# Two-layer gated cross-attention with routed experts: the steps of layer 0's attention dealt anew over four units, the pick split in two

## The reference, cut to what matters

```python
def reference(x, ctx, g_xattn, g_ffn, ...):     # x 32 x 128 x 128, ctx 32 x 77 x 128, float32
    x = x + tanh(g_xattn[0]) * xattn0(layernorm(x), ctx)   # 8 heads of 64
    x = x + tanh(g_ffn[0])   * ffn0(layernorm(x))          # 8 experts, the best 2 of each token
    x = x + tanh(g_xattn[1]) * xattn1(layernorm(x), ctx)   # 16 heads of 8
    x = x + tanh(g_ffn[1])   * ffn1(layernorm(x))          # 8 experts, the best 2 of each token
    return x

def xattn0(x, c):
    q, k, v = x @ Wq, c @ Wk, c @ Wv
    return softmax(q k^T / 8) v @ Wo + bo                  # for each head

def ffn0(x):
    scores = x @ Wr.T + br
    w, (_, idx) = softmax(scores), top_k(scores + biases_N, 2)
    ...
```

## Time and profile before

| | |
|---|---|
| median of 3 runs | 753.79 us (753.32 to 755.35) |
| the profiled execution | 752.22 us, span 750.5 us |
| mean granted clock of PE | 0.934 of full speed |
| busy: PE, PEld | 629.7 (84%), 571.5 (76%) |
| busy: DVE, ACT, POOL | 557.5 (74%), 444.4 (59%), 448.3 (60%) |
| chain that ended last | PE 37%, DVE 27%, ACT 13%, issue 10%, POOL 6%, DMA 4%, SP's queue 3% |

### The profile page before, as it was taken

One profiled execution on the slowest core, in us unless ns is written; L12 is line 12 of the kernel. 1 busy time (PEld: TensorE's weight loads), 2 busy tenths in 40 slices (PEclk: granted clock), 3 DMA queues, 4 the chain that ended last, 5 costly groups with the idle time before them and its releaser, 6 DMA issues.

```text
span 750.5 us, 16523 instructions
## 1 busy us (share of the span) xinstructions
PE 629.7 (84%) x4501; PEld 571.5 (76%) x4501; DVE 557.5 (74%) x1971; ACT 444.4 (59%) x1275; POOL 448.3 (60%) x665
## 2 busy tenths in 40 slices
PE   6889787878776869998778998898879986799997
PEld 4668687868766869898767787787877876689885
DVE  3368688787876797997887888988868765455784
ACT  2477676766634546665657686677665742344462
POOL 4034347776766877886563435677656763766761
PEclk9599999999977899999989999999989995799999
DMA  9446667544523335335534533625414003333555
GB/s 258 132 116 163 179 169 201 140 115 129 146 76 93 93 102 154 104 101 156 146 100 102 126 96 70 137 78 103 120 34 117 25 28 87 101 93 100 148 167 162
DMA packets 127383, 89.48 MB, mean 119 GB/s; under 512 B 30996, under 2 KB 116276, under 8 KB 127260
## 3 DMA queue, kind: packets, MB, share of 16 engines
q1 hardware_dynamic: 110844, 64.93, 34.1%
q0 software_dynamic: 8128, 17.65, 7.2%
q10 hardware_dynamic: 8320, 5.85, 2.8%
HBM read 50.73 MB, written 39.85 MB: 121 GB/s over the span
## 4 chain that ended last, share of the span: by engine, by line
PE 37%; DVE 27%; ACT 13%; issue 10%; POOL 6%; DMA 4%; SPq 3%; DVEq 1%; ACTq 0%; POOLq 0%
PE banks L1162 8%; PE banks L1181 5%; PE banks L1025 4%; DVE row_max L1418 3%; POOL x_rows L1905 3%; PE banks L905 2%; SPq L815 2%; ACT prob L1294 2%; PE banks L968 2%; DVE prob L1421 2%; DVE x_res L1754 2%; PE banks L1010 2%; DMA v_rows<-vo 2%; ACT xm L1287 2%; POOL y_rows L1912 1%
## 5 line engine op out<-in xcount | busy, mean ns | idle before, releaser
L1912 POOL DMA_INDIRECT y_rows<-y_sb,result_at x134 | 131.0, 978 | 61.6 <-issue 24.6
L1162 PE MATMUL banks<-xb,up 128*128 128x128 f32 x820 | 123.4, 290 | 22.5 <-DVE hidden L1730 11.4
L1905 POOL DMA_INDIRECT x_rows<-xm,row x120 | 120.4, 1003 | 32.5 <-issue 27.5
L1162 PEld LDWEIGHTS banks<-xb,up 128*128 128x128 f32 x820 | 110.5, 203 | 32.7 <-issue 14.2
L1867 POOL TENSOR_TENSOR v_flat<-v_raw,row_head 104x64 f32<-104x64 f32 (+1 forms) x128 | 55.8, 464 | 73.1 <-ACT v_raw L1335 72.7
L1319 ACT ACTIVATE prob_t<-banks 128x512 f32<-128x512 f32 x192 | 73.3, 439 | 27.6 <-PE banks L992 27.6
L1025 PE MATMUL banks<-v_flat,prob_t 128*128 128x108 f32 (+2 forms) x640 | 86.9, 285 | 2.6 <-issue 1.7
L1025 PEld LDWEIGHTS banks<-v_flat,prob_t 128*128 128x128 f32 (+1 forms) x640 | 80.6, 199 | 9.6 <-ACT prob_t L1319 5.8
L1181 PE MATMUL banks<-down,hidden 128*128 x536 | 84.9, 283 | 0.1
L1833 POOL TENSOR_TENSOR prob<-prob,inv_sum 128x616 f32<-128x616 f32 x32 | 39.1, 1221 | 58.7 <-DVE inv_sum L1481 58.6
L1181 PEld LDWEIGHTS banks<-down,hidden 128*128 128x128 f32 x536 | 73.6, 199 | 0.5 <-issue 0.5
(11 more groups left out here) (238 smaller groups left out, 1630.4 us busy)
## 6 DMA issues: line engine op xcount, KB each, us to landing
vo_flat<-v_rows SPq DMA_DIRECT2D x32, 256.0 KB
x_norm<-x_rows SPq DMA_DIRECT2D x74, 72.0 KB
v_rows<-vo SPq DMA_DIRECT2D x38, 128.0 KB
x_far<-x_rows SPq DMA_DIRECT2D x60, 72.0 KB
gathered<-y_rows ACTq DMA_DIRECT2D x32, 128.0 KB
q_rows<-up_raw SPq DMA_DIRECT2D x8, 512.0 KB, 2.8
q_even<-q_rows SPq DMA_DIRECT2D x12, 256.0 KB
q_odd<-q_rows SPq DMA_DIRECT2D x12, 256.0 KB
```

Source lines behind the costliest of these rows:

```text
L1162: done = pe.matmul(banks[:, UP_BANK[i % 2], part * P:(part + 1) * P], block_w[:, i % WR, part // 2, part % 2 * P:(part % 2 + 1) * P], xb[: ...
L1905: pool.indirect_dma_start(out=x_rows[layer][:, :], out_offset=bass.IndirectOffsetOnAxis(ap=row[:, n, c:c + 1], axis=0), in_=xm[:, i % 2, j ...
L1912: pool.indirect_dma_start(out=y_rows[layer][:, :], out_offset=bass.IndirectOffsetOnAxis(ap=result_at[:, i % (2 * YR):i % (2 * YR) + 1], ax ...
```

## The change

It does three things, all in the plan; no instruction is added or taken away.

1. `prepare_attention0_at`: the key blocks of a group are dealt 3, 3, 2, 0 over turns 0 to 3 (they were 3, 2, 1 and, ahead of them, 2 in the turn 3 before). xt comes last in turn 2 instead of in its second place. The norm of a group goes from turn 0 to turn 2 of the group before, normalize from turn 1 to turn 3.
2. `value_halves`: the unit of each four that makes two half blocks of values is now turn 3 and no longer turn 2.
3. `route_tasks`: every group has steps of its own, and `pick` is cut in two. Its second half is `count`: DVE's hot vectors, their sum and the counts, and POOL's two products. In layer 0, mnorm, mnormalize, mturn, route and pick of groups 0 to 4 come one unit later, count one after pick, rank and the scatters two units later than before (the scatters of the groups 3 and 4 are then pressed into two units). Groups 5 to 7 and all of layer 1 keep their units, with count right behind pick.

So turn 0 then has three k0, mnormalize and count; turn 1 three k0, rank, mturn and a scatter; turn 2 two k0, xt, norm, route, lead and two scatters; turn 3 two value halves, normalize, pick, mnorm and a scatter. The tables of group 4 (totals, blocks, block_bias) go from units 27, 28 and 29 to 29, 30 and 31.

```diff
     at = {}
-    usual = steps[0]
     for g in range(NG):
         u = spacing * g + lag
-        steps_of = steps[g - NG + 4] if NG - 3 <= g < NG - 1 else usual
-        for kind, step in zip(("mnorm", "mnormalize", "mturn", "route", "pick", "rank", "lead"), steps_of[0]):
+        steps_of = steps[g]
+        for kind, step in zip(("mnorm", "mnormalize", "mturn", "route", "pick", "count", "rank", "lead"), steps_of[0]):
...
-        n = min(max(2 * (last + 1), (5 * (u + 1) + 13) // 4), 2 * CTX_BLOCKS)
+        n = min(max(2 * (last + 1), (5 * (u + 1) + 12) // 4), 2 * CTX_BLOCKS)
...
     g = (u + 1) // GS + 1 if u >= GS - 1 else 1
-    if g >= NG:
-        return [], [], [], []
-    keys = ((3, 2, 1, 2) if g > 1 else (3, 3, 2, 0))
     turn = u % GS
-    before = sum(keys[i] for i in ((3, 0, 1, 2) if g > 1 else (0, 1, 2))[:(turn + 1) % GS if g > 1 else turn])
-    places = [[("k0", g, before + n)] for n in range(keys[turn])]
-    if turn == 2:
+    keys = (3, 3, 2, 0)
+    places = [[("k0", g, sum(keys[:turn]) + n)] for n in range(keys[turn])] if g < NG else []
+    if turn == 2 and g < NG:
         places.append([("xt", g)])
     places += [[]] * (3 - len(places))
-    return places + [[("norm", g)] if turn == 0 else [("normalize", g)] if turn == 1 else []]
+    norms = [("norm", 1)] if u == 0 else [("normalize", 1)] if u == 1 else []
+    if turn == 2 and g + 1 < NG:
+        norms = [("norm", g + 1)]
+    if turn == 3 and g < NG:
+        norms = [("normalize", g)]
+    return places + [norms]
...
-            if late and late[0] == ("expert_w",):
+            if late and late[0][0] in ("count", "expert_w"):
...
-    tasks = [route_tasks(0, GS, 6, ((range(7), (5, 6, 7, 8)), (range(7), (5, 6, 7, 8)), ((0, 1, 2, 3, 3, 4, 5), (5, 5, 5, 5)))),
...
+    tight = ((0, 1, 2, 3, 4, 4, 5, 6), (5, 6, 7, 8))
+    spread0 = (1, 2, 3, 4, 5, 6, 7, 8)
+    steps0 = [(spread0, (7, 8, 8, 9))] * 3 + [(spread0, (7, 7, 8, 8))] * 2 + [tight, ((0, 1, 2, 3, 3, 3, 4, 5), (5, 5, 5, 5)), tight]
...
+    tasks = [route_tasks(0, GS, 6, steps0), route_tasks(1, 2 * GS, 13, steps1)]
...
+                elif kind == "count":
+                    layer, g = t[1:]
+                    i = layer * NG + g
+                    s = i % 2
+                    w.wait_ge("top_idx", (GS + 1) * (i + 1))
+                    w.wait_ge("constants", N_CONSTANTS)
                     iota3 = iota8[:, :].unsqueeze(1).to_broadcast([P, GS, NEXP])
                     for n in (0, 1):
                         dve.tensor_tensor(hot[:, s, n, :, :], iota3, top_idf[:, s, :, n:n + 1].to_broadcast([P, GS, NEXP]),
...
-                elif kind == "pick" and t[1] == 0:
+                elif kind == "count" and t[1] == 0:
```

More of the change, by code:

```diff
@@ L361, in order @@
     out += first[1:] + [("wvo", 0), ("wvo", 1), ("ctx", 1), ("v0", 0, 0), ("v0", 0, 1), ("gates",)]
-    tasks = [route_tasks(0, GS, 6, ((range(7), (5, 6, 7, 8)), (range(7), (5, 6, 7, 8)), ((0, 1, 2, 3, 3, 4, 5), (5, 5, 5, 5)))),
-             route_tasks(1, 2 * GS, 13, (((0, 1, 3, 5, 6, 7, 9), (9, 11, 13, 15)), ((0, 1, 3, 5, 6, 7, 9), (8, 9, 10, 11)),
-                                         ((0, 1, 2, 3, 4, 5, 6), (6, 6, 7, 7))))]
+    tight = ((0, 1, 2, 3, 4, 4, 5, 6), (5, 6, 7, 8))
+    spread0 = (1, 2, 3, 4, 5, 6, 7, 8)
+    steps0 = [(spread0, (7, 8, 8, 9))] * 3 + [(spread0, (7, 7, 8, 8))] * 2 + [tight, ((0, 1, 2, 3, 3, 3, 4, 5), (5, 5, 5, 5)), tight]
+    spread1 = (0, 1, 3, 5, 6, 6, 7, 9)
+    steps1 = [(spread1, (9, 11, 13, 15))] * 5 + [(spread1, (8, 9, 10, 11)), ((0, 1, 2, 3, 4, 4, 5, 6), (6, 6, 7, 7)), (spread1, (9, 11, 13, 15))]
+    tasks = [route_tasks(0, GS, 6, steps0), route_tasks(1, 2 * GS, 13, steps1)]
     after0 = [[("expert", 1, e)] for e in range(NEXP)] + first_keys_and_queries()
```

## The result

Slower, and by three times what was forecast: 778.08 us (median of 6 runs, 775.75 to 781.78) against 753.56 for the kernel before on the same chip, ratio 1.0327 [1.0287, 1.0367]. That is +24.5 us where +8.0 stood, outside the range (748 to 767). The profiled execution took 781.78 us with a span of 780.0; it is the slowest of its six, so differences of the traces run a little high (29.6 us against 24.5).

A forecast was written before the change was run, and what follows sets the result against it. Layer 0's attention was taken to run at VectorE's pace plus its waiting gaps. Terms +8.6 (units 12 to 26), 0, -1.4 and +0.8 made +8.0 us on 752.22: 760.2, stated as a 761.5 median, range 748 to 767.

The forecast's parts named there:

- The mechanism of turn 1: Layer 0 attention, turn 1: late exponentials, third key block, then rank and mturn in bank 7; 5.3 to 7.95 us, +2.7.
- its rows are read 0.73 later ... and row_max comes 1.51 later: Turn 1, units 17 and 25: rank from 5.9, read 0.73 later, mturn at 6.9, row_max 1.51 later, at 8.4 us.
- Turn 2: Layer 0 attention: two key blocks, xt's low half, norm, route and lead; 7.4 to 7.25 us, -0.15 a group.
- Turn 0: Layer 0 attention: no late start of ACT, count and shift added; -1.25 us a group, then +0.7 for POOL.
- The wait for POOL's power: Turn 0: normalize's shift waits for POOL's power until 6.35 us after row_max, where 5.65 was wanted; +0.7 a group.
- an exclusive lock: VectorE and GpSimd's shared ports: rank gains outside POOL's divide; 761.5 us by this rule, 765.5 without it.
- Turn 3: Layer 0 attention: loses key blocks, rank and mnormalize, gains pick and mnorm; 5.2 to 5.55 us, +0.3 a group.
- Units 2 to 11: Early units with little or no routing: gains and losses cancel, 0 us, between -3 and +2.
- Units 27 to 30: End of the stage: same work, lighter units 27 and 28 close a fifth of the idle time; -1.4 us.
- The term for block_bias in unit 31: Block_bias comes ahead of rank on PE and in bank 7; its read and one rank cost +0.8 us.
- Closing gaps: Rival: PE and ACT run ahead in lighter turns 3 and 0, turn 1 5.9 us; 746 to 751.5 us, chance 0.25.
- POOL falling behind: Rival: late divides hold PE's turning of the probabilities, 1.5 us more a group; 767 us, chance 0.1.

The follow-up runs named there:

- second trace of the changed kernel: The changed kernel run again unaltered, on the other kind of chip: 829.9 us against 803.3 for the kernel before, ratio 1.0323.
- the split kernel: Kernel before with only the count taken out of the pick, same steps, count right behind it: 801.4 us against 802.7, ratio 1.0008.
- norm late: Changed kernel with the shifting and scaling of xm moved behind the following unit's exponentials: 822.0 us, ratio 1.0241 to the kernel before.
- rank late: Changed kernel with rank, turning, totals and blocks moved behind the following unit's scores and exponentials: 820.3 us, ratio 1.0197 to the kernel before.
- filling the first stand: Changed kernel with the transposes of the probabilities made three times over in turn 1, nothing moved: 824.9 us, ratio 1.0249 to the kernel before.
- cutting the second: Changed kernel with layer 0's turning, route and rank in the bank the last split did not use: 825.3 us, ratio 1.0272 to the kernel before.

## Why the prediction was wrong

- *The mechanism of turn 1* was right to a few tenths: exponentials 2 us late, rank at 5.71 in the heavy unit (forecast 5.9), the chain rank, turning, scores, and 17 and 25 longer than 13 and 21. **The step that failed is "its rows are read 0.73 later ... and row_max comes 1.51 later".** These prices were taken from rows at full clock. In the place where I put them they measured 1.23 and 2.66 at half clock, so 1.65 more a unit, 6.6 in four units; turn 1 came out 6.1 above the forecast (38.0 for units 13, 17, 21 and 25, forecast 31.9). The rows on record did not say that the clock would fall: 0.73 was measured behind a stand of 2.92 us and 1.51 behind one of 1.26, both at full clock, and the 0.84 of unit 12 comes from its first 2 us. But the same trace has unit 23, where PE stands 2.88 us ahead of the rank, and the scores behind it run at half clock. Windows of before, in units 12, 15 and 23:

```profile
107.92:109.92 2.00, 2.00 (x11) 2.00 (x11) 1.27 (x4) 1.88 (x6) 1.38 (x2) 0.50 0.67 202
131.90:133.67 1.77, 1.77 (x14) 1.77 (x15) 0.94 (x6) 0.00 (x0) 1.23 (x2) 1.00 0.04 8
182.00:184.06 2.06, 2.06 (x9) 2.06 (x9) 0.92 (x5) 0.69 (x2) 1.23 (x3) 0.50 0.70 188
```

  So a second sum at half clock was called for, and was not made.
- *Turn 2*: 8.0 us in the mean instead of 7.25, 3.0 in four units. It begins at half clock (unit 18: 0.51 from 161.98 to 163.60, 1.00 behind it): x_res waits for the weighted sum four times, 3.3 us in all.
- *Turn 0*: 7.34, 7.81 and 7.34 instead of 6.45, 3.1 us. The wait for POOL's power was forecast at 0.7 and measured 0.94 to 1.1. Here the forecast's sum is wrong in itself: 6.4, 1.7, 2.7 and 1.5 make 12.3 and not 12.1, and less the 5.55 of turn 3 that is 6.75 after turn 0's row_max, 1.1 late. What I left out is that m_shift then begins 0.04 us after POOL's divide and ends with it, 1.18 us instead of the 0.15 it takes alone; the forecast has 0.1 for it. The Trainium skill (SBUF — State Buffer, "SBUF: two separate sides"), weighed in the forecast, calls the shared port pair an exclusive lock; the trace agrees, here as for the rank (rank_hot 0.23 outside a divide, 1.29 under one). I used it where it speaks for the change and did not look which instruction came under the divide in exchange. The run with the norm moved got these 2 us back in turn 0.
- *Turn 3* at 5.25 to 5.45 (forecast 5.55) and unit 12 at 5.63 (6.45) were no loss, together 1.3 better. 6.1 + 3.0 + 3.1 - 1.3 = 10.9 is what the stretch took beyond the forecast (19.4 less 8.6 is 10.8).
- *Units 2 to 11*, put at 0 with +2 as the upper end, cost 8.6 (6.4 in the second trace of the changed kernel). Unit 9 took 8.38 instead of 7.4 with half clock again (0.80; in the second trace 7.22), unit 7 10.16 instead of 8.05, where PE stands 5.62 us for the loads of values and goes on at half clock, unit 8 6.76 instead of 4.9; units 3, 10 and 11 are longer than before by 1.05, 1.28 and 0.95. "The rest is small both ways" was not worked out from any row of SyncE's queue, and that was the mistake.
- *Units 27 to 30* took 29.0 us instead of 28.84 - 1.4: 4.53 and 5.38 in units 27 and 28, 8.82 and 10.27 in 29 and 30, where the tables meet pick, count and mnorm. The lighter two gave back just what the heavier two took, and not the fifth of the idle time that I let them close; the clock was 0.77 and 0.83 in the last two. The term for block_bias in unit 31, +0.8, measured 1.2 up to the first gate.
- *The rivals.* Closing gaps is refuted by every turn 1. POOL falling behind showed as m_shift's wait and also as its rival said: PE's turning of the probabilities waits for POOL's divide six times, 3.4 us in 15 units, where 1.5 a group would be 5.6; whether that is on the path no run took apart. The rival that was missing is the same order at a lower clock.

**What the runs settle.** Most of what layer 0's attention loses is of placement against dealing: with the routing taken out from between two scores the stage is back nearly whole (unit 31 at 236.5 against 258.4, the split kernel 235.4), but 1.3% of the 3.2% is still lost, at the seam behind the stage. It is not one wait: taking the head (norm late), the tail (rank late) or the bank wait away alone moved the stand to the next unit or the next step. The half clock is 1.65 us of each turn 1, by the durations of the same instructions, 6.6 us in the four of units 12 to 26. Why the clock falls in one unit and not in another stays open: filling the first stand did not keep it, cutting the second brought the fall forward, and in the kernel before one stand of 2.9 us left it full and another did not.
